# Aggregating a graph layer's float32 rows as three bf16 products on TensorE

## The reference, cut to what matters

```
xn   = layernorm(x)
msg  = xn[src]                                     # 100000 rows of 256
agg  = segment_sum(msg, dst, num_segments=6250)
deg  = segment_sum(ones, dst)
h    = relu(layernorm'(x) @ W_self + (agg / max(deg, 1)) @ W_neigh + b)
```

## Time and profile before

| What | us |
|---|---|
| median of three runs | 2617.11 |
| the profiled execution, by its own time | 2615.68 |
| span of its trace | 2613.9 |
| `prepare` and what is ahead of it | 0 to 107 |
| aggregation, first to last gather | 107.6 to 1315.3 |
| busy: TensorE | 1948.9 (75%) |
| busy: GpSimd | 1478.5 (57%) |
| busy: VectorE | 1195.9 (46%) |
| busy: ScalarE | 884.9 (34%) |
| DMA, mean rate | 108 GB/s |

### The profile page before, as it was taken

How to read it: one execution, slowest core, us unless ns; L and a number is a source line. 1 busy time by engine, 2 the same in 40 slices (tenths; PEclk the granted TensorE clock), 3 DMA queues, 4 the chain that set the end, 5 groups by cost and what they waited for, 6 DMA issues and landing times. The chain is left out here.

```text
span 2613.9 us, 26780 instructions
## 1 busy us (share of the span) xinstructions
PE 1948.9 (75%) x7528; PEld 1340.9 (51%) x7528; DVE 1195.9 (46%) x2204; ACT 884.9 (34%) x1904; POOL 1478.5 (57%) x1512
## 2 busy tenths in 40 slices
PE   4698888877778787765557888888879888883236
PEld 3555555554455555544446555555546565552223
DVE  6353333356455454533376323224245153356279
ACT  3433444454434353443224111322213223222124
POOL 2366666666666665666612666666767666660600
PEclk9799999898888888876766899999899999896555
DMA  5443333444444343453358321221222212215554
GB/s 181 141 150 120 89 87 89 117 123 137 118 125 135 110 147 109 127 184 89 97 181 278 102 51 34 65 47 37 58 51 58 51 37 67 44 37 188 156 166 145
DMA packets 197052, 282.87 MB, mean 108 GB/s; under 512 B 43024, under 2 KB 147444, under 8 KB 195763
## 3 DMA queue, kind: packets, MB, share of 16 engines
q0 software_dynamic: 61280, 115.13, 17.8%
q1 hardware_dynamic: 97218, 121.11, 14.1%
q10 hardware_dynamic: 38416, 44.96, 5.2%
HBM read 195.29 MB, written 85.80 MB: 108 GB/s over the span
## 5 line engine op out<-in xcount | busy, mean ns | idle before, releaser
L864 POOL DMA_INDIRECT ag_msg<-xn_tab,step_src x784 | 779.9, 995 | 429.3 <-issue 222.7
L1831 POOL DMA_INDIRECT edge_rows<-hx_d,gat_src x648 | 627.3, 968 | 315.2 <-issue 187.0
L1132 PE MATMUL ag_ps<-ag_msg,ag_hot 128*128 x1760 | 513.9, 443 | 151.5 <-POOLq L850 74.4
L1132 PEld LDWEIGHTS ag_ps<-ag_msg,ag_hot 128*128 128x128 f32 x1760 | 376.8, 222 | 289.4 <-issue 228.0
L2021 PE MATMUL ex_psY<-co_rows 128*128 128x256 f32 x1568 | 399.5, 411 | 86.8 <-issue 66.6
L886 DVE TENSOR_TENSOR acc<-acc,ag_ps 128x257 f32 x440 | 186.0, 423 | 561.3 <-PE ag_ps L1132 237.8
L2021 PEld LDWEIGHTS ex_psY<-co_rows 128*128 128x128 f32 x1568 | 319.2, 207 | 161.3 <-issue 93.5
L2006 PE MATMUL ex_psF<-co_rows 128*128 128x448 f32 x896 | 367.2, 564 | 41.9 <-issue 19.4
L1311 ACT ACTIVATE gat_self<-iota_row,step_nloc 128x128 f32<-128x128 f32 x880 | 272.6, 388 | 322.0 <-DVE xnT L910 132.7
L1945 DVE TENSOR_TENSOR hi_one_low<-hi_numbers,hi_low 128x2048 bf16<-128x2048 f32 x64 | 146.4, 2288 | 470.5 <-remote 382.9
L2006 PEld LDWEIGHTS ex_psF<-co_rows 128*128 128x128 f32 x896 | 174.3, 198 | 219.3 <-issue 197.0
(11 more groups left out here) (384 smaller groups left out, 1976.4 us busy)
## 6 DMA issues: line engine op xcount, KB each, us to landing
y_d<-co_rows ACTq DMA_DIRECT2D x28, 896.0 KB
co_rows<-y_d SPq DMA_DIRECT2D x28, 896.0 KB, 9.7
ag_msg<-xn_tab,step_src POOLq DMA_INDIRECT x784
xnT<-base_d SPq DMA_DIRECT2D x7, 1792.0 KB, 12.5
edge_rows<-hx_d,gat_src POOLq DMA_INDIRECT x648
base_d<-xnT ACTq DMA_DIRECT2D x7, 1024.0 KB
sums_d<-edge_rows SPq DMA_DIRECT2D x5, 1344.0 KB
xg<-in_x_dram SPq DMA_DIRECT2D x7, 896.0 KB, 5.8
```

The lines of the kernel that those rows point to most:

```text
L864: pool.indirect_dma_start(msg[:, b % RING, u, 0:D], None, c.xn_tab, bass.IndirectOffsetOnAxis(ap=t.idx[:, at:at + 1], axis=0)).then_inc(s_ ...
L1132: last = nc.tensor.matmul(bank[(at + r) % BANKS][:, 0:ROWW], hot[:, k, v0 + r * JOIN + j, :], ring[:, j * ROWW:SLOTS * ROWW][:, ds(places[ ...
L1831: pool.indirect_dma_start(G[:, j % RING, w, :], None, c.hx_d, bass.IndirectOffsetOnAxis(ap=plan.idx[:, at + w:at + w + 1], axis=0)).then_i ...
```

## The change

A row of the table becomes three bf16 parts that sum to the float32 value: high (the rounded value), middle (the rounded remainder) and low (the rounded remainder of that), stored in the order middle, low, high. A row has 1536 bytes instead of 1024. In `prepare`, TensorE puts the results of two tiles side by side in one bank (three or four banks instead of two); ScalarE copies a pair as the high part; VectorE subtracts it from PSUM (`remainders`, four instructions a group); ScalarE rounds the remainder as the middle part (`middles`, two a group); VectorE subtracts again to give the low part (`lows`, two a group). The remainders, the order test and the keys lie in `acc`, which GpSimd therefore clears in three pieces, the last after the last low part. In `aggregate` the one-hots are bf16, the ring's rows have 770 bf16 columns, and each float32 product becomes three bf16 products into the same bank: high with its two columns of ones (257 columns read), middle and low (256 each).

```
+                def remainders(g):
+                    v.drain()
+                    for f, (u0, n) in enumerate(PAIRS):
+                        v.wait_ge(s_parts, first_part(g, f))
+                        V.tensor_tensor(left[:, u0:u0 + n, :], bank(g, f)[:, 0:n * D].rearrange("p (u d) -> p u d", u=n),
+                                        part[:, g % 2, u0:u0 + n, HI:HI + D], ALU.subtract).then_inc(s_tabs, 1)
+                def lows(g):
+                    for i, (u0, n) in enumerate(HALF):
+                        v.wait_ge(s_parts, second_part(g, i))
+                        V.tensor_tensor(part[:, g % 2, u0:u0 + n, D:2 * D], left[:, u0:u0 + n, :],
+                                        part[:, g % 2, u0:u0 + n, 0:D], ALU.subtract).then_inc(s_tabs, 1)
...
-                pe.wait_ge(s_dec, 1)
+                pe.wait_ge(s_t, 1)
+                pe.wait_ge(s_tabs, first_part(GROUPS - 2, NP - 1))
...
-                    for u in range(GT):
-                        n = g * GT + u
-                        act.wait_ge(s_tab, n + 1)
-                        A.copy(tab[:, g % 2, u, :], psT[n % 2][:, 0:D]).then_inc(s_tabs, 1)
+                    for f, (u0, n) in enumerate(PAIRS):
+                        act.wait_ge(s_tab, g * NP + f + 1)
+                        A.copy(part[:, g % 2, u0:u0 + n, HI:HI + D],
+                               bank(g, f)[:, 0:n * D].rearrange("p (u d) -> p u d", u=n)).then_inc(s_parts, 1)
+                def middles(g):
+                    for i, (u0, n) in enumerate(HALF):
+                        act.wait_ge(s_tabs, first_part(g, 2 * i + 1))
+                        A.copy(part[:, g % 2, u0:u0 + n, 0:D], left[:, u0:u0 + n, :]).then_inc(s_parts, 1)
...
-                        pool.indirect_dma_start(msg[:, b % RING, u, 0:D], None, c.xn_tab,
+                        pool.indirect_dma_start(msg[:, b % RING, u, 0:PARTS * D // 2], None, c.xn_tab,
...
-                                last = nc.tensor.matmul(bank[(at + r) % BANKS][:, 0:ROWW], hot[:, k, v0 + r * JOIN + j, :],
-                                                        ring[:, j * ROWW:SLOTS * ROWW][:, ds(places[r], ROWW)],
-                                                        start=(j == 0), stop=(j == JOIN - 1))
+                                for to, n in ((HI, ROWW), (0, D), (D, D)):
+                                    last = nc.tensor.matmul(bank[(at + r) % BANKS][:, 0:n], hot[:, k, v0 + r * JOIN + j, :],
+                                                            ring[:, j * MSGW + to:SLOTS * MSGW][:, ds(places[r], n)],
+                                                            start=(j == 0 and to == HI), stop=(j == JOIN - 1 and to == D),
+                                                            skip_group_check=True)
```

## The result

The changed kernel takes 2677.6 us in the median of 4 runs (2675.8 to 2694.6), the kernel before 2616.2 us on the same chip (2609.6 to 2618.1). The ratio is 1.026, with a 95% interval of 1.0235 to 1.0284: slower, by 61 us where 20 were forecast. The time lies within the stated range of 2550 to 2710 and on the side that was thought likelier.

What follows compares the result with a forecast made beforehand. GpSimd's gathers were taken to bound the aggregation. A span of 2613.9 + 17 (`prepare`) - 12 (TensorE) + 10 (landings) + 5 (longer gathers) = 2633.9 us, with 1.8 us around it 2636 us; range 2550 to 2710.

Steps and rivals of the forecast that it cites:

- the bound: Aggregation: follows GpSimd's gathers, not TensorE's busy time; 784 gathers of 946 ns plus 0.30 us gap, at least 980 us.
- `prepare`, +17 us: Stage before the first gather: VectorE's 31 us of new work partly fills idle time; +17 us, between +10 and +28.
- the aggregation (+3, measured 25.6): First to last gather: products -12, later landings +10 and longer gathers +5, forecast together as +3 us.
- the upper bound for the decoding: In `prepare`: VectorE's decoding for TensorE comes 24.5 us later if no idle time takes new work, 7 if all does.
- The landings, +10: Aggregation: each batch of longer rows lands 0.23 us later, mostly within slack; +10 us, 45 if all 196 batches waited.
- longer gathers, +5 us: Aggregation: gathers beside bulk transfers, 38 us over the usual time, lengthen with half as many bytes again; +5 us, 0 to +19.
- TensorE, -12 us: Aggregation's products: a quarter shorter, about 128 us less busy time, mostly hidden behind gathers; -12 us, gain between 0 and 40.
- The price of a product: TensorE in the aggregation: a 256-column bf16 matmul takes 133 ns, three make 0.40 us against 0.53 for a float32 product.
- The rival of the clock: TensorE: less work lowers its granted clock, other work lengthens, the gain vanishes; 2648 us, counted within the forecast's 0.60.
- The addresses, 0 us: TensorE's queue: two more address instructions per product, 1760 x 46 ns = 81 us, hidden behind the gathers; 0 us.
- Completions: Rival, aggregation: quicker products make TensorE's completions come sooner, freeing the ring earlier; half of 194 us waits gone, 2551 us; chance 0.24.
- Bound by issue: Rival, aggregation: TensorE limited by issuing matmuls with addresses, 207 ns each, threshold 0.17; 2733 us; chance 0.16.

Runs made afterwards that it cites:

- the longer rows alone: Kernel before with table, ring and gathers 1536 bytes wide, float32 products kept, added bytes unread; four runs on prompt chips, ratios 1.0094, 1.0079, 1.0087, 1.0101.
- the short rows: Changed kernel gathering only middle and low parts (1024 bytes), high part a constant in the ring; 2333.6 us, ratio 1.0140 to the kernel before.

## Why the forecast was wrong in size

The direction was right, and so was the bound. Two parts of the sum were mis-sized: `prepare` (+17, measured 31.2) and the aggregation (+3, measured 25.6). In the first a step failed; in the second a slack was read as an average.

**The bound** held: the aggregation follows the gathers, 946 ns and a 0.30 us gap each, before and after.

**`prepare`, +17 us**, came out at 31.2, beyond its own upper end of 28. VectorE's new work was sized right (27 us measured, 31 reckoned), and so was the use of its old idle time, of which some 18 us went. The step that failed is the one that gave remainders and low parts no waits of their own, except behind the last table: "most of the idle time was spent on other engines' results of groups whose remainders can be done meanwhile". They wait for ScalarE's parts, 24.0 us of it ahead of the last table, and they stand ahead of the next rows, so that these waits closed a loop over three engines. Another order took 12.7 us of it away again, with the waits for middle parts (from 21.8 to 10.1 us). That the last table moved by 24.5 us, the very number of the upper bound for the decoding, is chance: the bound meant 24.5 us of work and no idle time used, and what came was 22.1 us of work and 2.4 of idle time. From the last table on it was sized at 3.5 us more and took 6.7 more. Of these 6.7, 2.0 are the table at a slower clock (0.76 for 1.00), and some 4.7 are remainder, middle and low parts with the store.

**The landings, +10, and longer gathers, +5 us.** By the longer rows alone these 15 us came out at 16 to 24, by the short rows at 24 to 27, on prompt chips, inside their bounds. The gathers themselves did not get longer (780.5 us busy against 779.9, and on prompt chips 786.8 against 794.1), so it is all landings. What was wrong is that the slack was read as an average. Most batches do have slack: 152 of 196 wait no longer than 0.55 us. But where the bulk transfers fill the DMA engines a batch that waits does so for some 2.8 us, and the longer rows made more batches wait, there and elsewhere (44 instead of 30 over 0.55 us). The mean DMA share of the aggregation in the earlier trace rows (0.43) hides these places; a window of 8.5 us shows 1.0. They account for 10 of the 22 us, so the picture covers the growth only in part. Nor did the gathers of over 1.0 us lie where bulk transfers run, as the forecast's +5 had it: in the trace before, the DMA share beside them is 0.45 on average and 0.44 beside the others, while 90 of these 130, but only 171 of the other 653, run for 0.3 us or more beside a two-input operation of 128x512 on VectorE. That is a coincidence in time, and no run tests it.

The Trainium skill (DMA: Bandwidth & Descriptors, "Anatomy of one DMA") gave an estimate of 29 us for 196 exposed landings; the 16 to 24 us measured with the longer rows alone lie under it, and they fell unevenly on the batches.

**TensorE, -12 us**, was about right where it could be measured: -4 to -9 us on prompt chips, near the spread of single executions. There TensorE waits 245.1 us for GpSimd before its products, so saving work on it can gain little. On the chip of the comparison no run measures the term. The price of a product was right for its clock and wrong for the average: at a granted clock of 0.96 a matmul takes 0.139 us (forecast 0.133), over the whole aggregation of the comparison 0.165, at clocks of 0.66 to 0.90. The forecast's 128 us of saved busy time did not follow from 0.133 either: 2640 x 0.133 = 351 us is 163 less than 513.9, since a float32 instruction took 0.292 us on average and not the 0.266 of one stretch. Measured were 77. The rival of the clock was right in its direction (0.96 to 0.90, and 7% more for the other matmuls). The 109 ns that I cited from the Trainium skill (TensorE: Matmul & The Clock Gate, "Back-to-back issue gap") for a warm matmul lies under the 139 measured at 0.96 and further still under the 165.

**The addresses, 0 us**: 46 ns each in the middle as before; nothing in the runs points to them.

**Rivals.** *Completions* did not come sooner: "remote" and TensorE's part together went from 164.6 to 165.9 us, with 102 waits of over 0.55 us instead of 80. That TensorE's work does weigh on a late chip was right in it, though: one product instead of three took 50 us off there. *Bound by issue* had its threshold, 0.17 us a matmul, too low, because it counted the two register loads of 1.19 us for a pair of rounds on the new side alone, though the old side has them too. At 0.165 us nothing of it shows on prompt chips, where TensorE waits for GpSimd. *Still open* is how the 25.6 us of the comparison divide between bytes and products on a late chip, since the longer rows alone never got one. On prompt chips it is all bytes. The traces of the comparison point the same way without proving it: of the 25 us by which the waits before gathers grew, 15 stand beside stretches of 4 us or more in which the DMA engines were full, and 5 in gaps of under 0.55 us, much as on prompt chips.

## What to carry to other kernels

Before work is put into an engine's idle time, ask what the new work itself waits for: if it needs other engines' results, it brings waits along, and ahead of the step that starts the next round these waits close a loop. Put new work behind what the next round needs, and give each new step its own wait in the sum until the order is shown to allow less. For a transfer's slack don't take the mean; look at short windows for bulk transfers that fill the DMA engines, and place a landing check as late as the buffers allow: here one gather's time was worth 1.0 to 1.5% on prompt chips without any other change.

## What the runs showed of the hardware

- The same kernel took 2616 and 2635 us on some chips and 2300 to 2307 on others, 12% less. Part of the difference lies in waits for TensorE's completions: GpSimd waits 164.6 us before the aggregation's gathers for L1132 or "remote" on the chip of the comparison, 2.4 us on a prompt chip, and the aggregation takes 1207.7 and 1091.0 us.
- A third of the product work made the changed kernel 2% faster on a late chip and some 0.7% slower on a prompt one, by the ratios to the kernel before; on the prompt one at a granted clock of 0.84 instead of 0.96 from 230 to 532 us, with 0.347 us instead of 0.292 for each of the other matmuls.
- The same table of 28 matmuls took 6.21 us at a granted clock of 1.00 and 8.19 us at 0.76, where TensorE had been without work for 4.1 us shortly before; single matmuls of it followed each other every 0.22 us, and every 0.43 us at the lower clock.
- An indirect gather of 128 rows kept GpSimd for the same 946 ns (median) with rows of 1024 and of 1536 bytes, and for 944 ns with 96 bytes.
- The DMA share was 0.98 to 1.04 over 8.5 us, at 326 to 333 GB/s, when 2.1 MB of direct transfers met the gathers, with 1024 and with 1536 bytes a row.
